# Layer 3 cross attention of a fused decoder: maxima from row scores, joined by a product to second scores with the keys in rows

## The reference, cut to what matters

```python
q = (x @ Wq + bq).reshape(B, N, 16, 16)
k = (y @ Wk + bk).reshape(B, M, 16, 16)
v = (y @ Wv + bv).reshape(B, M, 16, 16)
scores = einsum('bnhd,bmhd->bhnm', q, k) * 0.25
attn = softmax(scores, axis=-1)                     # over the 375 keys
out = einsum('bhnm,bmhd->bnhd', attn, v).reshape(B, N, 256)
h = relu(out @ W1 + b1)
return h @ W2 + b2                                  # then x = layernorm(x + .)
```

## Time and profile before

| | |
|---|---|
| median of 3 runs | 1793.6 us (1793.58 to 1795.64) |
| span of the profiled execution, first to last instruction | 1785.6 us; the runs are 8.0 us longer than it |
| PE busy, DVE, ACT, POOL | 1579.5 (88%), 941.3 (53%), 717.5 (40%), 409.0 (23%) us |
| layer 3 cross attention, from its first scores to the columns of its last rows | 1351.67 to 1546.37 us |
| its transposes of probabilities (L1268) | 384, busy 53.9 us |
| its exponentials on ACT (L2053) | 128, busy 72.0 us |
| its score copies with maxima on DVE (L2897) | 128, busy 63.3 us |
| its copies of turned tiles (L2906 DVE, L2063 ACT) | 64 and 32, busy 37.6 and 17.0 us |

### The profile page before, as it was taken

How to read it: one execution, slowest core, us unless ns; L and a number is a source line. 1 busy time by engine, 2 the same in 40 slices (tenths; PEclk the granted TensorE clock), 3 DMA queues, 4 the chain that set the end, 5 groups by cost and what they waited for, 6 DMA issues and landing times.

```text
span 1785.6 us, 40853 instructions
## 1 busy us (share of the span) xinstructions
PE 1579.5 (88%) x14786; PEld 1305.9 (73%) x14786; DVE 941.3 (53%) x2546; ACT 717.5 (40%) x1675; POOL 409.0 (23%) x627
## 2 busy tenths in 40 slices
PE   7998998799987879998797788997988999899998
PEld 6876776678975657776687566775876777689897
DVE  3665877511116657777110562556345667565864
ACT  3334876232323336652222314551755556211110
POOL 2224776500004421112000233432121111000101
PEclk9998999999998999998899798998998999999999
DMA  5343000278951011102686001001001000033232
GB/s 212 147 151 121 28 27 19 106 279 300 321 185 35 1 53 44 29 15 87 254 290 228 13 1 58 28 27 48 1 1 66 23 26 15 24 96 117 81 108 68
DMA packets 41852, 166.72 MB, mean 93 GB/s; under 512 B 5985, under 2 KB 16865, under 8 KB 30177
## 3 DMA queue, kind: packets, MB, share of 16 engines
q1 hardware_dynamic: 39392, 159.14, 25.7%
q0 software_dynamic: 2304, 5.51, 1.0%
HBM read 140.21 MB, written 24.41 MB: 92 GB/s over the span
## 4 chain that ended last, share of the span: by engine, by line
PE 70%; DVE 12%; issue 7%; DMA 3%; POOL 3%; ACT 3%; SPq 1%; DVEq 0%; POOLq 0%; ACTq 0%
PE bank L1688 7%; PE bank L1701 6%; PE bank L1268 6%; PE bank L1630 4%; PE bank L1255 4%; PE bank L1631 4%; PE bank L1632 4%; PE bank L1282 3%; PE bank L795 2%; PE bank L804 2%; PE bank L1238 2%; PE bank L1243 2%; PE bank L896 1%; PE bank L782 1%; DMA xrow<-slots 1%
## 5 line engine op out<-in xcount | busy, mean ns | idle before, releaser
L2053 ACT ACTIVATE arena<-big,nm 112x375 f32<-112x375 f32 x384 | 215.9, 605 | 29.5 <-DVE nm L2894 16.4
L1268 PEld LDWEIGHTS bank<-cst,arena 112*125 112x125 f32 x1152 | 146.6, 192 | 54.0 <-issue 29.0
L1268 PE MATMUL bank<-cst,arena 112*125 112x112 f32 x1152 | 168.0, 283 | 8.8 <-ACT big L2063 5.0
L3150 POOL TENSOR_TENSOR mv<-mv,cst 112x1 f32<-112x1 f32 x88 | 20.1, 228 | 607.3 <-DVE mv L2283 607.3
L2202 ACT ACTIVATE htile<-bank,wup 128x128 f32<-128x128 f32 x280 | 79.7, 368 | 189.7 <-PE bank L1688 189.6
L1688 PE MATMUL bank<-xtile,wup 128*128 128x128 f32 x1120 | 132.8, 278 | 0.3 <-DVE xtile L2997 0.2
L1688 PEld LDWEIGHTS bank<-xtile,wup 128*128 128x128 f32 x1120 | 129.8, 194 | 1.0 <-DVE xtile L2997 0.9
L3013 DVE COPY yrow<-bank 128x256 f32<-128x256 f32 x35 | 14.8, 424 | 217.5 <-PE bank L1701 217.5
L1701 PE MATMUL bank<-wdn,htile 128*128 128x256 f32 x560 | 126.3, 379 | 0.0
L2897 DVE TENSOR_SCALAR_CACHE_REDUCE big<-bank 112x375 f32<-112x375 f32 x192 | 96.0, 543 | 35.3 <-PE bank L1255 33.6
L1701 PEld LDWEIGHTS bank<-wdn,htile 128*128 128x128 f32 x560 | 103.9, 190 | 12.8
(11 more groups left out here) (359 smaller groups left out, 3571.7 us busy)
## 6 DMA issues: line engine op xcount, KB each, us to landing
wup<-in_moe_up SPq DMA_DIRECT2D x35, 1028.0 KB, 7.3
wdn<-in_moe_dn SPq DMA_DIRECT2D x35, 1024.0 KB, 6.1
vspace<-in_ring SPq DMA_DIRECT2D x40, 512.0 KB, 4.2
ctxs<-parts SPq DMA_DIRECT2D x30, 564.0 KB, 3.9
slots<-mlpw SPq DMA_DIRECT2D x11, 1024.0 KB, 6.5
parts<-ctxs SPq DMA_DIRECT2D x8, 564.0 KB, 3.1
xrow<-slots SPq DMA_DIRECT2D x35, 128.0 KB, 5.0
slots<-yrow SPq DMA_DIRECT2D x35, 128.0 KB, 7.0
```

The source lines that it names most:

```text
L1268: mm = pe.transpose(bank[4 + (3 * g + t) % 2][0:KT, j * T:(j + 1) * T], c_pr[:, g, j, t * KT:(t + 1) * KT], ident[0:T, 0:T])
L2053: nc.scalar.activation(c_pr[:, g, j, :], c_sc[:, g % 2, j, :], ACT.Exp, bias=nm[:, p, h:h + 1], scale=-1.0).then_inc(cexp_done, 1)
```

## The change

In layer 3's cross attention `joined` takes the place of `cross` on every engine. The row scores are kept only for their maxima: DVE reduces two banks at a time (8 reductions per batch). The 16 maxima of a row are split into a rounded part and a remainder, laid out in four strips, turned by one transpose and spread by DVE to a 128 x 448 tile that holds, in each strip, the negated maxima of its four heads. Second scores have the keys in rows: for each third of the keys and each strip, a product of ones with that tile starts the sum and two products of keys and queries add to it. ACT takes the exponentials straight out of PSUM into the layout that the values read. No score copies, transposes of probabilities or tile copies are left.

The PSUM banks are shared in another way: banks 0 to 5 are three pairs, taken in turn by everything except the small products of bank 7. A pair is taken again when the engine that read its last use is done (`wait_turn`). The programs run a batch apart: in pass b, the row scores and value rows of b+1, the second scores and values of b, the keys and queries of b+2 and the output of b-1. On POOL a pass is `residual_rows(b)`, `ln_root(b - 1)`, `spread(b + 2)`, `keep_rows(b - 1)`. The loop is written out, where `cross` had a loop of pairs of batches. Beside that three semaphores are joined with others (`consts_in` and `x_in`; `first_in` into `mlp_in`), and a table of 4 columns is added to the constants. The pieces below are, in this order, the turns of the banks, PE's products and its passes, ACT's exponentials and passes, and DVE's reductions and passes.

```diff
+    def rota(self):
+        order = [("K", 0, 0)]
+        for b in range(-1, B):
+            for g in range(GROUPS):
+                if b + 1 < B:
+                    if g == 3:
+                        order.append(("V", b + 1, 0))
+                    order.append(("R", b + 1, g))
+                if b >= 0 and g < 3:
+                    order.append(("T", b, g))
+            if b + 2 < B and b + 2 > 0:
+                order.append(("K", b + 2, 0))
+        self.turn_of, self.turns = {}, []
+        for use in order:
+            for half in range(2 if use[0] in "RT" else 1):
+                self.turn_of[use + (half,)] = len(self.turns)
+                self.turns.append(use + (half,))
...
+        def wait_turn(eng, sub, k):
+            if k < 3:
+                return
+            kind, b, x, half = sub.turns[k - 3]
+            if kind == "R":
+                eng.wait_ge(amax_done, at(sub, "n4", b, 2 * x + half + 1))
+            elif kind == "T":
+                eng.wait_ge(ap_done, at(sub, "s4", b, 4 * x + 2 * half + 2))
+            elif kind == "K":
+                eng.wait_ge(ck_done, at(sub, "c2", b, 2))
+            else:
+                eng.wait_ge(cv_done, at(sub, "c3", b, 3))
...
+                def two_banks(kind, b, x, half):
+                    k, first = turn_banks(sub, kind, b, x, half)
+                    wait_turn(pe, sub, k)
+                    return [bank[first], bank[first + 1]]
...
+                def scores(b, g, p):
+                    out = two_banks("R", b, g, 0) + two_banks("R", b, g, 1)
+                    if g == 0:
+                        pe.wait_ge(cqm_ready, at(sub, "c1", b, 1))
+                        pe.wait_ge(ck_done, at(sub, "c2", b, 2))
+                    for i in range(4):
+                        rows = slice(32 * i, 32 * i + 32)
+                        mm = pe.matmul(out[i][0:T, 0:S2], c_qm[rows, p, g // 2, g % 2, :], c_kT[rows, p, g // 2, :],
+                                       start=True, stop=True)
+                        if i % 2:
+                            mm.then_inc(as_ready, 1)
...
+                def scores_t(b, t, p):
+                    out = two_banks("T", b, t, 0) + two_banks("T", b, t, 1)
+                    if t == 0:
+                        pe.wait_ge(anm_done, at(sub, "n1", b, 1))
+                    for i in range(4):
+                        rows = slice(32 * i, 32 * i + 32)
+                        pe.matmul(out[i][0:KT, 0:4 * T], ones_k[rows, :], j_nT[rows, :, :].rearrange("p j n -> p (j n)"),
+                                  start=True, stop=False)
+                    for ch in range(2):
+                        for i in range(4):
+                            rows = slice(32 * i, 32 * i + 32)
+                            mm = pe.matmul(out[i][0:KT, 2 * T * ch:2 * T * ch + 2 * T], c_kT[rows, p, ch, t * KT:(t + 1) * KT],
+                                           c_qm[rows, p, ch, :, :].rearrange("p e n -> p (e n)"), start=False, stop=(ch == 1))
+                            if ch == 1:
+                                mm.then_inc(at_ready, 1)
...
+                for b in range(-1, B + 1):
+                    p = b % 2
+                    now, ahead, far, back = 0 <= b < B, b + 1 < B, b + 2 < B, 0 <= b - 1
+                    if ahead:
+                        scores(b + 1, 0, 1 - p)
+                    if back:
+                        if now:
+                            pe.wait_ge(anm_done, at(sub, "n1", b, 1))
+                        if b >= 2:
+                            pe.wait_ge(xt_done, xt_at(sub, b - 2))
+                        output_rows(sub, b - 1)
+                    if now:
+                        scores_t(b, 0, p)
+                    if back:
+                        output_columns(sub, b - 1)
+                    if ahead:
+                        scores(b + 1, 1, 1 - p)
+                    if back:
+                        filler(0 if now else 2)
+                        hidden(b - 1)
+                    if now:
+                        scores_t(b, 1, p)
+                    if ahead:
+                        scores(b + 1, 2, 1 - p)
+                    if back:
+                        filler(0 if now else 2)
+                        project_out(b - 1)
+                    if now:
+                        scores_t(b, 2, p)
+                    if ahead:
+                        value_rows(b + 1, 1 - p)
+                        scores(b + 1, 3, 1 - p)
+                    if far:
+                        keys(b + 2, p)
+                        if back:
+                            pe.wait_ge(ln_dve, START + 3 * ln_unit(sub, b - 1) + 1)
+                        elif not now:
+                            pe.wait_ge(cq_done, at(sub, "c1", 0, 1))
+                        q_in(b + 2, p)
+                    if ahead:
+                        if far:
+                            pe.wait_ge(cq_done, at(sub, "c1", b + 2, 1))
+                        maxima(b + 1)
+                    if now:
+                        values(b, p)
+                    if back:
+                        filler(0 if now else 4)
+                        if ahead:
+                            pe.wait_ge(anm_done, at(sub, "n1", b + 1, 1))
+                        rows_t(sub, b - 1, 1 - p)
...
+                def exps(b, t):
+                    for i in range(4):
+                        first = turn_banks(sub, "T", b, t, i // 2)[1]
+                        act.wait_ge(at_ready, at(sub, "s4", b, 4 * t + i + 1))
+                        nc.scalar.activation(j_pT[:, t, i, :], bank[first + i % 2][0:KT, 0:4 * T], ACT.Exp).then_inc(ap_done, 1)
...
+                    if now:
+                        exps(b, 0)
+                    if back:
+                        hidden(b - 1)
+                    if now:
+                        exps(b, 1)
+                        exps(b, 2)
+                    if ahead:
+                        value_rows(b + 1, 1 - p)
+                    if far:
+                        keys(b + 2, p)
+                        q_in(b + 2, p)
+                    if back:
+                        rows_in(B + sub.base["row"], b - 1)
...
+                def maxima(b, g):
+                    for half in range(2):
+                        first = turn_banks(sub, "R", b, g, half)[1]
+                        dve.wait_ge(as_ready, at(sub, "n4", b, 2 * g + half + 1))
+                        dve.reduce_max(j_max[:, 2 * half:2 * half + 2, g], banks[0:T, first:first + 2, 0:S2], AX_X, negate=True)\
+                            .then_inc(amax_done, 1)
...
+                    if back:
+                        output_in(sub, b - 1, cpv_done, at(sub, "c4", b - 1, 4))
+                    if ahead:
+                        maxima(b + 1, 0)
+                    if back:
+                        output_normed(sub, b - 1)
+                        output_columns(sub, b - 1)
+                    if ahead:
+                        maxima(b + 1, 1)
+                        maxima(b + 1, 2)
+                    if back:
+                        residual(sub, b - 1, 1 - p)
+                        stats(sub, b - 1, 1 - p, 0)
+                    if ahead:
+                        maxima(b + 1, 3)
+                        maxima_split(b + 1)
+                    if back:
+                        rows_out(sub, b - 1, 1 - p)
+                    if ahead:
+                        maxima_in(b + 1)
+                    if b in (B - 2, B - 1):
+                        for j in range(2):
+                            split_weights(2 * (b - B + 2) + j, 2 * (b - B + 2) + j)
```

More of the change, by code:

```diff
@@ L293, in decoder @@
             c_pr = take(T, 4, 4, S2)
+            take = carve(arena, "arena joined")
+            take(128, 448 + 896 + 256 + 448)
+            j_pT = take(KT, 3, 4, 4 * T)
+            take(128, 4 * T)
+            j_nm = take(T, 4, 32)
+            j_max = take(T, 4, 4)
             take = carve(arena, "arena cross norm")
@@ L407, in decoder @@
             kv = shared("kv", [128, 2, 4 * DM], F32R)
-        bank = [ctx.enter_context(nc.psum_tensor(f"bank{i}", [128, 512], F32)) for i in range(8)]
+        banks = ctx.enter_context(nc.psum_tensor("bank", [128, 8, 512], F32))
+        bank = [banks[:, i, :] for i in range(8)]
         OT, TL = bank[6], bank[7]
@@ L1809, in _ @@
                 elif isinstance(sub, Cross):
-                    (cross_normed if sub.qk_norm else cross)(sub)
+                    (cross_normed if sub.qk_norm else joined if sub.joined else cross)(sub)
                 elif sub.index in (2, 5):
@@ L3340, in cross, with joined, spread @@
                 cross_steps(pool, step, 8 if sub.mlp else 7)
+            def joined(sub):
+                def spread(b, p):
+                    pool.wait_ge(cq_done, at(sub, "c1", b, 1))
+                    for m in range(2):
+                        ins = nc.gpsimd.tensor_tensor(c_qm[:, p, m, :, :], c_q[:, p, m, :].unsqueeze(1).to_broadcast([128, 2, T]),
```

(15 more changed lines are left out.)

170 lines of the change are left out of this document (149 added, 21 removed).

## The result

The changed kernel takes 1813.75 us (median of 7 runs, 1799.85 to 1818.36), the kernel before 1793.58 beside it (7 runs, 1789.63 to 1798.06): 1.0104 times as long, 95% interval 1.0077 to 1.0131. I had forecast 1799.2 us. The sign holds; the loss is 20.2 us where I had 5.6. The profiled execution took 1818.36 us with a span of 1816.5, so its stages are read by themselves, each from its own first instruction.

The account below looks back on a forecast made before the run. PE was taken to set the time, busy 109.97 of 116 us. Losses of 1.7 us (start), 0.2 (five passes) and 3.8 (end) made 5.6 us, so 1793.6 + 5.6 = 1799.2 us; range 1786 to 1815.

Parts of the forecast that it names:

- The full passes: Passes b = 1 to 5: six steps between row scores and second scores sum to 23.34 us, against 23.31 before.
- five passes: 0.2 lost: Five full passes in steady state: together 0.2 us slower than before.
- The signs that I named: Period near 23.3 us; PE idle before row scores (2 to 2.5 us a pass), first second scores and turned maxima.
- Start and end: First and last passes of the stage: 1.7 us lost at the start, 3.8 at the end.
- the ones strip by strip: Rival, second scores: four strips of ones run one after another, 0.66 us more per group, 1815 us; 10%.
- The clock falls: Rival: PE's short waits lower its clock to 1.2 GHz for a fifth of the stage, 17 us, 1816 us; 6%.
- The splits: Passes 6 and 7: moved weight splits on DVE's queue make the copy of the values 2.1 us late each time.
- PE's work alone counts: Rival, full passes: waits are hidden, a pass takes 19.4 us, the kernel 1768; 12%, 3% more for shorter chains.
- The splits do no harm: Rival, passes 6 and 7: values end later than counted, so 1795 to 1797 us, no change to be told; 10%.
- The joined semaphores: Start of the kernel: joining them costs nothing; without cover, the later of two loads, once.

Follow-up runs that it names:

- e2: Changed kernel plus 16 products of no use ahead of the waits of passes -1 and 0; 1799.25 us, 1.0039 times the kernel before.
- e8: Changed kernel, splits left in place, plus products of no use ahead of waits in passes -1 and 0 and 6 to 8; 1793.68 us, ratio 1.0018.
- e3: Changed kernel with the product of ones issued twice, the second over the first; 1809.39 us, 1.0094 times the kernel before.
- e1: Changed kernel with the four weight splits moved behind the columns of the turned output in passes 7 and 8; 1801.28 us, ratio 1.0047 to the kernel before.
- e7: Changed kernel run once more, unchanged, as a control; 1815.19 us, 1.0090 times the kernel before.
- e4: Changed kernel with both the moved splits and the 16 products of no use in passes -1 and 0; 1790.35 us, 0.9988 times the kernel before.
- e5: As e4, with half of the MLP's second layer put ahead of the third row scores; 1789.11 us, 0.9978 times the kernel before.
- e6: As e5, with the values put ahead of the turned maxima in pass 6 alone; 1784.50 us, 0.9938 times the kernel before.

## Why the prediction came out as it did, step by step

**The full passes: right, and a little better.** Forecast 1.89, 2.48, 2.80, 2.48, 2.74 and 10.95 us; measured, from the rows above, 1.98 (1405.65 to 1407.63), 2.35, 2.80, 2.38, 2.74 and 10.66. The 0.43 us less come mostly from ACT. Four of its exponentials take 1.85 us at 1408.86, where layer 2's took 2.21:

```profile
1408.86 1.85 ACT L2356 ACTIVATE arena<-bank 125x448 f32<-125x448 f32 x4 [5.94 <-PE bank L1577]
```

They start 1.23 us after the ones; I had 1.27. The reductions, a form that the trace of before did not have, take 936 ns; I had 0.93. (The four of 448 elements in 2.22 us scale to 0.93 for 750 as well, not to the 0.90 that I wrote; only 0.93 stands in the sum.)

```profile
L3229 DVE TENSOR_REDUCE arena<-bank 112x2 f32<-112x750 f32 x64 | 57.2, 936 | 72.1 <-PE bank L1557 72.1
```

The term "five passes: 0.2 lost" is 2.0 us gained (114.53 against 116.54). Its core held: PE's work gets shorter, and the waits give nearly all of it back.

The signs that I named are there in part. PE is idle for 3.1 us a pass, where I had 3.9; ahead of row scores, with ACT's exponentials as releaser, for 0.52 + 1.15 = 1.67 us, under my 2 to 2.5; ahead of the turned maxima for 0.69, behind ACT's query copy. The 0.45 us ahead of the first second scores have no releaser ("issue"), which I had called a sign of another cause. By its length it is still the reduction: the step takes 1.98 us for my 1.89, and in pass 0, with nothing laid over it, the same wait ahead of the next second scores has DVE's reduction as releaser (1.11 us at 1387.57).

**The step that failed: "Start and end", for the clock at which it was priced.** Both were summed with durations from stretches at 1.00. At that clock they are right: 33.7 for 33.9 in e2, 50.2 for 49.75 in e8. In the changed kernel the start takes 40.3 and the end 57.1 us. Of the 17.2 us in the stage, e8 leaves 3.8 to the chain of waits and the splits; 13.4 are the clock. So the sign came out for a reason that I held unlikely. By the chain alone, as in e8, the kernel would be 2.4 us slower, which can't be told from no change. It was also luck that 1813.75 us lies inside the range of 1786 to 1815: the range left the fall of the clock out, and its upper end was the time of another rival, the ones strip by strip. The changed kernel's second median, 1815.19, lies just beyond it.

**The rival "The clock falls" was the right mechanism in the wrong place.** I judged it by the full passes, where PE would be idle for a sixth, and by a row of layer 1 with 14% idle at 1.00. For the full passes that was right: 14% idle, clock 1.00. But my own sum for the start had passes with nothing to lay over the waits, and I never asked the question there. PE stands a quarter of the start idle. I gave the rival 6% and priced it for a fifth of the stage at 17 us; half the clock in parts of start and end cost 13.4. The Trainium skill, "TensorE: Matmul & The Clock Gate", section "A second HAM failure mode: psum-queue depth-cycling", warns of swings between both clocks through small idle gaps while PSUM banks are cycled; I set it aside. The start bears it out (0.55, 0.95, 0.52 in the windows after each other, no gap over 1.2 us), and the full passes, which cycle through the same banks, do not.

**The splits: right as waits, undersized in what they set off.** 2.1 us late twice, as forecast (2.3 and 2.2). That two such waits behind a third (2.40 us for the maxima) would halve the clock for the work behind them was not in the sum.

**The other rivals.** Strip by strip falls by e3. "PE's work alone counts" falls: with all clocks at 1.00 a pass still has 15.4 / 5 = 3.1 us of idle PE. "The splits do no harm" falls by e1. The joined semaphores could not be told apart: PE's first product starts at 7.29 us before and 7.77 after, but at 7.05 in e8 and 8.36 in e2.

**What stays open.** The stage explains 17.2 us; the medians differ by 20.2, and in e7 by 22. In the other variants the change of the stage and that of the median (the kernel before beside them at 1791.25 to 1793.24) agree within 2.3 us. The runs of the changed kernel spread over 1799 to 1819 us, and why its median lies 3 to 5 us above what its stage says was not settled. The spread goes with the granted clock of the whole launch: 0.950 in its shortest execution (1799.85 us), 0.938 to 0.940 in the three longest (1816.09 to 1818.36). In the two profiles it differs ahead of the stage too, where the program's work is the same: PE's records there add up to 1186.8 us in the changed kernel (mean clock 0.94) and to 1176.8 before (0.95). Whether the change has a part in that, no run shows.

## What to carry to other kernels

Before pricing a stretch with durations from a steady one, work out PE's idle share of that stretch by itself: first and last passes of a pipeline have the same waits and less work to lay over them, and here they fell to 1.2 GHz in part while the steady passes kept 2.4. A high share is a reason to look and no rule: e4's end is 19% idle at 1.00. When a chain measures longer than its sum, fill the waits with products of no use first: if the time falls, the clock was it. Other waits took real work instead, in e5 and e6; that the start's products can be replaced by such work, no run shows. Work moved onto an in-order queue is priced by who stands behind it and by what that wait does to PE's clock.

## What the runs showed of the hardware that I had not expected

- Products of no use made a chain of waits shorter: 16 of them, 6.6 us less (e2 against the changed kernel).
- The same gap does not always cost the clock. PE stands idle for 2.4 us ahead of the turned maxima of pass 6 in seven profiles; the values behind it take 2.51 us in four of them (the changed kernel twice, e4 and e5), 3.71 in e1, 4.02 in e3 and 4.17 in e2. Even the same code of the end comes out either way: e1 and e4 share it, and take 47.1 and 45.7 us.
- Four strips of 32 rows with 448 columns cost 0.20 us together where one product of 376 columns over the whole array takes 0.19.
